# Transposed activations emptied from PSUM two chunks at a time, and a new hand-written order of the five engines

## The reference

```python
def layer(h, params):
    wl, b_l, ws, b_s, wr, b_r, g, beta = params
    u = jnp.einsum('bid,bjd->bij', h, h) / temper
    a = jax.nn.softmax(u, axis=-1)
    delta = a * adjacency_matrix
    attn = delta / (jnp.sum(delta, axis=-1, keepdims=True) + 1e-10)
    hl = h @ wl.T + b_l
    hs = h @ ws.T + b_s
    hr = h @ wr.T + b_r
    diag_a = jnp.diagonal(attn, axis1=1, axis2=2)
    ctx = jnp.einsum('bij,bjd->bid', attn * upper, hl) + diag_a[..., None] * hs + jnp.einsum('bij,bjd->bid', attn * lower, hr)
    ...
    return (jax.nn.relu(o), None)
...
x = _layernorm(x + _L0_gnn_ref(x, adj, ...), axis=-1)
x = _layernorm(x + _L1_gnn_ref(x, adj, ...), axis=-1)
```

## Time and profile before

| | |
|---|---|
| median of 3 runs | 1866.24 us (1865.49 to 1866.89) |
| the profiled execution | 1864.76 us, of which the span of its instructions is 1863.0 us |
| busy share of the span | PE 93%, PEld 88%, DVE 83%, ACT 68%, POOL 35% |
| busy share of the DMA engines, in slices of the middle | mostly 6 or 7 tenths |
| granted TensorE clock, mean | 0.977 of full speed |

### The profile page before, as it was taken

The page is one execution under the profiler, slowest core; times in us unless marked ns, Lnnn a source line. Parts: engine busy times, 40 slices in busy tenths (PEclk is TensorE's granted clock), DMA queues, the critical chain, the costliest instruction groups (busy, mean ns, idle before and its releaser), DMA issues.

```text
span 1863.0 us, 39868 instructions
## 1 busy us (share of the span) xinstructions
PE 1731.2 (93%) x13120; PEld 1633.3 (88%) x13120; DVE 1555.4 (83%) x5383; ACT 1267.5 (68%) x3036; POOL 652.9 (35%) x777
## 2 busy tenths in 40 slices
PE   4899999999999999999999999999999999999963
PEld 4799899999999999999999999899999999999952
DVE  4578889888888988888998888898888889888865
ACT  3466767676767776676767676676767776767644
POOL 1223333343333334343334333333434333433331
PEclk9899999999999999999999999999999999999975
DMA  5157666767666666766676776666666667677555
GB/s 156 29 106 149 127 130 131 145 135 147 145 122 132 136 143 141 150 134 125 132 144 139 143 144 124 129 137 145 138 151 136 123 135 140 138 143 144 115 116 116
DMA packets 550036, 247.65 MB, mean 133 GB/s; under 512 B 423100, under 2 KB 549832, under 8 KB 549832
## 3 DMA queue, kind: packets, MB, share of 16 engines
q1 hardware_dynamic: 538928, 231.91, 61.9%
q10 hardware_dynamic: 10904, 13.20, 2.1%
HBM read 56.25 MB, written 12.58 MB: 37 GB/s over the span
## 4 chain that ended last, share of the span: by engine, by line
PE 61%; DVE 24%; ACT 9%; issue 3%; DMA 1%; SPq 1%; ACTq 0%; POOL 0%; DVEq 0%; POOLq 0%
PE bank_w L384 33%; PE bank_m L384 10%; PE bank_u L384 6%; PE bank_o L384 4%; DVE halves L890 4%; DVE bank_s L885 4%; PE bank_s L384 4%; ACT normed L632 2%; ACT bank_s L683 2%; DVE stats_y L851 2%; ACT halves L692 2%; DVE hlrl L792 2%; DVE normed L848 2%; PE bank_t L401 2%; DVE attTl L797 1%
## 5 line engine op out<-in xcount | busy, mean ns | idle before, releaser
L683 ACT ACTIVATE bank_s<-bank_s,hmin 128x256 f32<-128x256 f32 x768 | 311.1, 445 | 129.8 <-DVE hmin L885 114.1
L885 DVE CUSTOM_DVE_ANT_0 bank_s<-bank_s,bias_adj 128x256 f32<-128x256 f32 x768 | 308.1, 446 | 40.7 <-PE bank_s L384 40.4
L890 DVE TENSOR_TENSOR halves<-bank_s,halves 128x512 f16<-128x512 f32 x384 | 262.3, 683 | 27.4 <-ACT halves L692 24.3
L692 ACT ACTIVATE halves<-bank_s 128x512 f16<-128x512 f32 x384 | 228.6, 596 | 4.2
L384 PE MATMUL bank_w<-w_graph0h,hT_ach 128*128 128x384 f32 x576 | 201.5, 350 | 10.3 <-DVE w_graph0l L745 6.0
L384 PE MATMUL bank_w<-w_graph1h,hT_bh 128*128 128x384 f32 x576 | 200.1, 347 | 0.0
L384 PE MATMUL bank_o<-v_parts,pT 128*128 128x99 bf16 (+1 forms) x3072 | 186.7, 204 | 12.6 <-DMA pT<-halves 9.3
L384 PE MATMUL bank_w<-w_graph0l,hT_ach 128*128 128x384 f32 x576 | 195.6, 340 | 0.0
L384 PE MATMUL bank_w<-w_graph0h,hT_acl 128*128 128x384 f32 x576 | 195.3, 339 | 0.0
L384 PE MATMUL bank_w<-w_graph1l,hT_bh 128*128 128x384 f32 x576 | 195.0, 339 | 0.0
L384 PE MATMUL bank_w<-w_graph1h,hT_bl 128*128 128x384 f32 x576 | 194.6, 338 | 0.0
(11 more groups left out here) (177 smaller groups left out, 5327.3 us busy)
## 6 DMA issues: line engine op xcount, KB each, us to landing
x_in<-in_x SPq DMA_DIRECT2D x64, 384.0 KB, 3.7
adj_in<-in_adj SPq DMA_DIRECT2D x96, 256.0 KB, 3.6
q_st<-qk_hi SPq DMA_DIRECT2D x256, 96.0 KB, 2.3
k_st<-qk_hi SPq DMA_DIRECT2D x256, 96.0 KB, 2.3
q_st<-qk_lo SPq DMA_DIRECT2D x128, 96.0 KB, 2.2
k_st<-qk_lo SPq DMA_DIRECT2D x128, 96.0 KB, 2.2
out<-result ACTq DMA_DIRECT2D x32, 384.0 KB, 3.8
pT<-halves SPq DMA_TRANSPOSE x384, 3.1
```

Of the source, the lines that this page charges most:

```text
L683: nc.scalar.activation(bank[:, i * S:(i + 1) * S], bank[:, i * S:(i + 1) * S], ACT.Exp, bias=hmin[:, i, k:k + 1], scale=-1.0).then_inc(s_p ...
L692: nc.scalar.activation(halves[:, k % SPLIT, :, 0, :], bank_s[k % 2][:, :].rearrange("p (i s) -> p i s", i=NT), ACT.Copy).then_inc(s_pt_hi, 1)
L885: ve.tensor_tensor_reduce(bank_s[k % 2][:, i * S:(i + 1) * S], bank_s[k % 2][:, i * S:(i + 1) * S], bias_adj[:, i, :], -SCALE, BIG, ALU.ad ...
L890: ve.tensor_tensor(halves[:, k % SPLIT, :, 1, :], bank_s[k % 2][:, :].rearrange("p (i s) -> p i s", i=NT), halves[:, k % SPLIT, :, 0, :], ...
```

## The change

First, `TURNS = ((0, 1), (2,))`: a turn has two pieces and no longer three. Piece 0 transposes chunks 0 and 1 into the whole of bank_t (four transposes), piece 1 transposes chunk 2 (two transposes). ScalarE's copy and VectorE's subtraction of piece 0 are one instruction of 512 columns each; for h the relus stay at 256 columns each, since scale and bias belong to a chunk, so piece 0 has four. All counts of the turn semaphores go by the number of pieces.

Second, ORDER is new for all five engines. The lists also begin at another point of the round, which moves nothing by itself. In TensorE's list turn_y.1 goes behind a_mix.0 and attend.6, the old turn_y.1 and turn_y.2 being one piece now. attend.7 goes behind q.0, b_proj.0 ahead of scores.0, scores.3 ahead of b_proj.4, a_proj.0 ahead of b_mix.1, and attend.0 and attend.1 behind b_mix.1. turn_h.0 goes ahead of attend.8 and attend.9. On SyncE b_x and a_adj go ahead of weights.0, k_stack.3 and k_stack.2 go back, and c_adj goes ahead of a_x. On GpSimd c_sum goes ahead of v.0, and v.1 behind q.2 and b_turn. On ScalarE b_out goes behind a_proj.5, weights.10 behind scores.10, c_apply behind a_scores.

```diff
+TURNS = ((0, 1), (2,))
...
-        turn_y.0-1 turn_y.1-1 a_mix.0-1 turn_y.2-1 attend.6-1 scores.10-1 a_mix.1-1 attend.7-1 q.0 q.1
...
+        a_proj.3-1 a_proj.4-1 a_proj.5-1 scores.8-1 attend.4-1 scores.9-1 attend.5-1 turn_y.0-1 a_mix.0-1
+        attend.6-1 turn_y.1-1 scores.10-1 a_mix.1-1 q.0 attend.7-1 q.1 q.2 scores.11-1 k.0 turn_h.0 k.1
...
+        def turned(hT, k):
+            return hT[:, TURNS[k][0]:TURNS[k][-1] + 1, :].rearrange("p c s -> p (c s)")
...
             def turn_y(t, k):
                 pe.wait_ge(s_y, NT * t)
                 if k == 0:
-                    pe.wait_ge(s_th_lo, NC * t)
+                    pe.wait_ge(s_th_lo, len(TURNS) * t)
                     if t != NB:
-                        pe.wait_ge(s_tx_lo, NC * (t + 1))
-                wait(pe, s_ty_lo, NC * (t - 1) + k)
-                for i in range(NT):
-                    last = nc.tensor.transpose(bank_t[:, i * P:(i + 1) * P], y_in[:, i, k * P:(k + 1) * P], ident[:, :])
+                        pe.wait_ge(s_tx_lo, len(TURNS) * (t + 1))
+                wait(pe, s_ty_lo, len(TURNS) * (t - 1) + k)
+                for n, c in enumerate(TURNS[k]):
+                    for i in range(NT):
+                        last = nc.tensor.transpose(bank_t[:, n * S + i * P:n * S + (i + 1) * P],
+                                                   y_in[:, i, c * P:(c + 1) * P], ident[:, :])
                 last.then_inc(s_ty_pe, 1)
...
-                nc.scalar.activation(hT_ac[0][:, k, :], bank_t[:, 0:S], ACT.Copy).then_inc(s_ty_hi, 1)
+                nc.scalar.activation(turned(hT_ac[0], k), bank_t[:, 0:len(TURNS[k]) * S], ACT.Copy).then_inc(s_ty_hi, 1)
...
-                for dst in (hT_b[0][:, k, :], bank_t[:, 0:S]):
-                    nc.scalar.activation(dst, bank_t[:, 0:S], ACT.Relu, bias=b1_col[:, k:k + 1],
-                                         scale=g1_col[:, k:k + 1]).then_inc(s_th_f, 1)
+                for n, c in enumerate(TURNS[k]):
+                    for dst in (hT_b[0][:, c, :], bank_t[:, n * S:(n + 1) * S]):
+                        nc.scalar.activation(dst, bank_t[:, n * S:(n + 1) * S], ACT.Relu, bias=b1_col[:, c:c + 1],
+                                             scale=g1_col[:, c:c + 1]).then_inc(s_th_f, 1)
...
-                ve.tensor_tensor(hT_ac[1][:, k, :], bank_t[:, 0:S], hT_ac[0][:, k, :], ALU.subtract).then_inc(s_ty_lo, 1)
+                ve.tensor_tensor(turned(hT_ac[1], k), bank_t[:, 0:len(TURNS[k]) * S], turned(hT_ac[0], k), ALU.subtract).then_inc(s_ty_lo, 1)
```

More of the change, by code:

```diff
@@ L54 @@
-        attend.1 b_mix.1 a_proj.0 a_proj.1 attend.2 a_turn.0 scores.6 attend.3""",
-    "act": """
[L56 to L62, removed]
@@ L63 @@
-    "dve": """
-        scores.7-1 b_resid.0-1 b_resid.1-1 b_norm2.0-1 weights.6-1 b_out.0-1 a_turn.0-1 weights.7-1 a_proj.4-1
-        scores.8-1 a_proj.5-1 turn_y.0-1 attend.5-1 scores.9-1 turn_y.1-1 weights.8-1 a_mix.0-1 scores.10-1
-        turn_y.2-1 weights.9-1 a_mix.1-1 h_norm.0 attend.7-1 q.0 h_apply.0 q.1 scores.11-1 weights.10-1 q.2
-        k.0 weights.11-1 turn_h.0 k.1 attend.9-1 k.2 turn_h.1 turn_h.2 attend.11-1 turn_x.0 v.0 scores.0 v.1
-        b_scores.0 turn_x.1 b_proj.0 weights.0 scores.1 b_proj.1 b_mask.0 scores.2 c_stat.1 weights.1 c_stat.0
-        c_norm.0 turn_x.2 weights.2 b_turn.0 c_apply.0 scores.3 b_proj.4 b_proj.5 scores.4 a_scores.0
-        weights.3 b_mix.0 a_mask.0 b_mix.1 b_norm.0 attend.1 b_apply.0 weights.4 scores.5 a_proj.0 a_proj.1
-        attend.3 weights.5 scores.6""",
+        attend.0-1 attend.1-1 a_turn.0-1 a_proj.1-1 scores.6-1 attend.2-1 a_proj.2-1 attend.3-1 scores.7-1
@@ new lines @@
+    "dve": """
+        a_mask.0-1 b_mix.1-1 b_norm.0-1 a_proj.0-1 attend.1-1 b_apply.0-1 weights.5-1 scores.6-1 a_proj.1-1
+        a_turn.0-1 attend.3-1 scores.7-1 weights.6-1 b_resid.0-1 b_resid.1-1 b_norm2.0-1 a_proj.4-1 b_out.0-1
+        weights.7-1 scores.8-1 a_proj.5-1 attend.5-1 scores.9-1 turn_y.0-1 weights.8-1 a_mix.0-1 turn_y.1-1
+        scores.10-1 weights.9-1 a_mix.1-1 h_norm.0 q.0 h_apply.0 q.1 weights.10-1 scores.11-1 q.2 attend.7-1
+        k.0 weights.11-1 k.1 attend.9-1 turn_h.0 k.2 turn_h.1 attend.11-1 v.0 turn_x.0 v.1 b_scores.0 c_stat.0
+        scores.0 c_stat.1 b_proj.0 scores.1 weights.0 b_proj.1 b_mask.0 weights.1 c_norm.0 scores.2 scores.3
+        turn_x.1 b_turn.0 weights.2 c_apply.0 b_proj.4 scores.4 b_proj.5 weights.3 a_scores.0 weights.4
+        b_mix.0 scores.5""",
@@ L72 @@
     "pool": """
[L73 removed]
+        v.1-1 b_apply.0-1 a_turn.0-1 q.0 c_sum.0 v.0 q.2 b_turn.0""",
     "sp": """
[L75 to L77 removed]
+        k_stack.3-1 weights.2-1 k_stack.2-1 weights.3-1 weights.4-1 weights.5-1 weights.6-1 c_adj.0 a_x.0
@@ L78 @@
+        weights.7-1 weights.8-1 weights.9-1 weights.10-1 weights.11-1 q_stack.0 k_stack.0 b_adj.0 k_stack.1
+        b_x.0 q_stack.1 q_stack.2 a_adj.0 weights.0 weights.1 q_stack.3""",
 }
@@ L340, in b_x @@
                 if t < NB:
[L341 removed]
+                    wait(sp, s_tx_pe, len(TURNS) * (t + 1))
                 else:
```

73 lines of the change are left out of this document (39 added, 34 removed).

## The result

| | before | after |
|---|---|---|
| median, us | 1866.02 (5 runs, 1864.75 to 1866.89) | 1858.13 (5 runs, 1855.45 to 1861.04) |
| ratio, 95% interval | | 0.9957 (0.9945 to 0.9969) |
| the profiled execution, us | 1864.76, span 1863.0 | 1858.13, span 1856.4 |
| granted TensorE clock, mean | 0.977 | 0.976 |
| even round in the middle, us | 54.83 | 54.72 |

The account below looks back on a forecast made before the run. Bound by TensorE's part, then VectorE's stretch, with a second path nearly tied: 37.21 + 16.80 + 0.14 = 54.15 us a round for 54.82. 0.67 x 32 = 21.4 us saved gives 1845 us, range 1814 to 1874.

Parts of the forecast that it names:

- its own measure: Whole kernel: 0.2%, some 4 us, is what a measurement can tell from no change; same meant 1862.5 to 1870 us.
- What bounds the kernel: One round of 54.82 us: 15.44 on VectorE, 0.14 to hand over, 39.24 on TensorE; a second path is as long.
- the second path: TensorE up to scores.0, then VectorE alone to the stretch's end; forecast 53.9 us a round, 0.2 under the first path.
- The merged copies and turn_y: Wide copies save VectorE 0.46 us a batch; turn_y.1's 1.34 us wait goes; VectorE's stretch from b_mix.1 becomes 16.80 us.
- The other moves I cost at nothing: Moves on SyncE and GpSimd, v.1 behind b_turn among them, cost 0, since their readers come late enough or moved back too.
- a delay of 0.3: On either of the two nearly tied paths, a delay of 0.3 us is paid in full.
- the signs that the prediction gave for being wrong: TensorE waiting at turn_h.1 or turn_x.0 for VectorE, at attend.0 or scores.3 for a transfer, or VectorE's stretch well over 17.
- I take this round for all 32: One middle round of 54.82 us stands for all 32, so 0.67 us saved a round gives 21.4 us.
- Filling and draining: Start and end of the program, where the pipeline fills and drains: left as they are, no change counted.
- The h turn: Rival: turn_h.0's four relus in a row on ScalarE hold TensorE, 1888 us; slower by this or another, 0.20.
- VectorE gives it back: Rival: VectorE's stretch runs 0.7 us longer because ScalarE's copies come late, 54.8 a round, 1866 us; chance 0.10.
- The rule that speaks against it: Skill's advice to break up ScalarE and VectorE instructions; the change does the reverse, so alone it would mean slower.

Follow-up runs that it names:

- e3: The changed kernel with GpSimd's v.1 moved back to right behind v.0, ahead of q.2 and b_turn: 1832.47 us, 0.9822 of the kernel before.
- e7: The changed kernel with VectorE's c_apply.0 moved from ahead of b_proj.4 to behind b_proj.5, GpSimd left alone: 1830.69 us, 0.9812 of the kernel before.
- e1: The merged turns of the change in the engine order of the kernel before: 1895.91 us, 1.0158 of the kernel before.
- e9: As e1, but h turned in three pieces, so only x and y are merged: 1867.52 us, 1.0010 of the kernel before.
- e12: As e7, but h turned in three pieces, x and y merged: 1862.39 us, 0.9980 of the kernel before.
- e13: As e7, but y turned in three pieces, x and h merged: 1897.01 us, 1.0173 of the kernel before.

## Why the prediction was right and wrong

**Direction and range** were right: 1858.1 in 1814 to 1874, faster by 0.43%. The size was not: 7.9 us for 21. And part of the hit is luck: without the uneven rounds of before (5.3 us), of which the prediction knew nothing, the time would have been some 1863, no different from before by its own measure.

**What bounds the kernel** held in the main: the path from a_mix.1 on TensorE to the addition of a_mix.0 on VectorE. e3 took 0.81 us off c_apply and the round fell by 0.80, e7 by 0.90. That the second path ties with it no run shows: the sum put it 0.2 under the first, and in e7 VectorE has a wait of 0.43 in it. On that path the sum also took one change of group off TensorE (0.09), where the lists have two fewer; the part measured 19.3 for 19.13. And the slices of the profile in which the granted clock is low are the first two and the last two (0.92, 0.87, 0.78, 0.51), not the first and the last two; no term hangs on it.

**The merged copies and turn_y** (parts 1 and 2) were right: the wait went from 43.6 us to 0.9, VectorE's stretch is 16.66 for 16.80. e3, in which only v.1 is moved back, has a round of 53.92 where the sum said 54.15.

**The step that failed** is "The other moves I cost at nothing". For GpSimd I wrote that v.1 falls behind b_turn and looked only at its reader, attend.0. I did not look at what VectorE does at the time that v.1 then runs. Its subtraction held the last instruction of c_apply for 0.89 us instead of 0.25, which cost 0.7 us at c_apply and a wait of 0.63 at b_mix.0, in both paths at once, so it was paid nearly in full, as the prediction itself said of a delay of 0.3: the even round gained 0.11 and not 0.67, and 0.56 x 32 = 17.9 of the 21.4 us were gone. The earlier trace rows could have warned: VectorE is busy nearly without a gap there, so GpSimd's work must run beside some instruction of it, and which one is a question of place. None of the signs that the prediction gave for being wrong came up; a wait at b_mix.0 was not among them.

**"I take this round for all 32"** failed the other way. Eight rounds of before were longer, 5.3 us in all, and b_proj.0 ahead of scores.0 removed that. From q.0 of round 4 to that of round 32 the kernel before took 1744.91 - 204.38 = 1540.53 us and after 1737.71 - 205.63 = 1532.08. That is 8.45 less, 28 x 0.11 = 3.1 in the even rounds and the rest in the uneven ones. Filling and draining, which I had left as they are, took 1.9 more: -8.45 + 1.9 = -6.6, and 1858.13 - 1864.76 is -6.6 too.

**The rivals.** The h turn did not hold TensorE in the change (turn_h.1 starts without a wait, relu waits 65.8 us), but e1 shows the mechanism at its place in the order of before, 28 us. "VectorE gives it back" is nearest to what happened; it named ScalarE as the cause and the stretch behind b_mix.1 as the place, and both were wrong.

**The rule that speaks against it.** Cutting up h made the kernel 28.4 us faster in the order of before (e1 to e9) and 31.7 slower in the new one (e7 to e12). The Trainium skill (Perfetto Trace Analysis, Optimizing Scalar/DVE Operations) says that, if ScalarE and VectorE are not saturated but make bubbles on other engines, breaking up instructions may allow work to be completed sooner; e9 agrees, e12 and e13 do not. The waits shown suggest what decides: in e1 v.0 waited behind the long piece, in e12 and e13 the next transposes waited behind the first short one. No run tests this apart.

## What to carry to other kernels

When a step of GpSimd is moved, list what VectorE does in the time it lands in, and keep its small instructions with two operands in SBUF (the on-chip memory in which all tiles but the banks lie) away from it, above all on the path that bounds. Merging pieces and reordering are one change: each half alone lost 30 and 97 us here, so a piece count should be tried with the order that gives it cover. And sum over rounds, not over one: uneven rounds show work without cover.
